# Experts fed in two batches, the first running through the last image's seam

## The reference, cut to what matters

```
x = x + conv(_ln_c(x))          # gate of three attentions: compressed, selected (top 16 blocks), windows 7x7
t = tokens(x)
t = t + ffn(_ln_t(t))
ffn(x):                         # N = 4096 tokens, D = 128, E = 8 experts, H = 512, TOP_K = 2
  logits = xt @ Wr + br
  top_p, top_idx = top_k(softmax(logits), 2);  weights = top_p / sum(top_p)
  xn = layernorm(xt)
  xe = xn * ln_g[e] + ln_b[e]
  h  = gelu(xe @ W1[e] + b1[e]);  y = h @ W2[e] + b2[e]
  out = sum over the two chosen experts of weight * y
```

## Time and profile before

| | us |
|---|---|
| median of three runs | 842.24 (840.95 to 847.28) |
| profiled execution, its own time | 840.26 |
| its span in the trace | 838.5 |
| PE busy | 666.8 (80%) |
| DVE busy | 514.0 (61%) |
| ACT busy | 418.8 (50%) |
| POOL busy | 239.5 (29%) |
| stretch of the expert tiles | 659 to 810 |
| PE busy in it | 146.72 of 151 |

### The profile page before, as it was taken

How to read it: one execution, slowest core, us unless ns; L and a number is a source line. 1 busy time by engine, 2 the same in 40 slices (tenths; PEclk the granted TensorE clock), 3 DMA queues, 4 the chain that set the end, 5 groups by cost and what they waited for, 6 DMA issues and landing times.

```text
span 838.5 us, 17744 instructions
## 1 busy us (share of the span) xinstructions
PE 666.8 (80%) x5228; PEld 500.0 (60%) x5229; DVE 514.0 (61%) x1719; ACT 418.8 (50%) x1238; POOL 239.5 (29%) x406
## 2 busy tenths in 40 slices
PE   2998899986889989688998966787631599999953
PEld 1684476654557556355755643553430599998952
DVE  4208378938857884875887568679763244444434
ACT  1327634663742554554356455326311388887842
POOL 3100043001013730201472010345015356565630
PEclk9999999997999999689999979957965799999985
DMA  9100000001000000000010170011022122222236
GB/s 315 58 1 26 1 6 1 2 1 51 2 1 5 27 27 6 21 0 2 5 33 20 34 195 0 4 37 42 2 76 64 48 64 63 69 63 63 63 128 219
DMA packets 34288, 38.63 MB, mean 46 GB/s; under 512 B 11668, under 2 KB 27044, under 8 KB 33956
## 3 DMA queue, kind: packets, MB, share of 16 engines
q1 hardware_dynamic: 28660, 26.77, 10.7%
q0 software_dynamic: 4416, 9.00, 3.0%
q10 hardware_dynamic: 1152, 2.10, 0.7%
HBM read 24.94 MB, written 13.98 MB: 46 GB/s over the span
## 4 chain that ended last, share of the span: by engine, by line
PE 52%; DVE 24%; issue 6%; ACT 6%; POOL 5%; DMA 4%; SPq 2%; DVEq 0%; POOLq 0%; ACTq 0%
PE ps L1919 7%; PE ps L1903 7%; PE ps L1483 6%; PE ps L1488 6%; PE ps L1537 5%; PE ps L1594 4%; DVE nmx L1060 4%; PE ps L1621 3%; DVE t_tok L1186 3%; DVE x_tok L1045 3%; PE ps L1552 3%; DVE r_P L1070 3%; PE ps L1524 2%; POOL xs_d L651 2%; DMA qTs<-z_d 2%
## 5 line engine op out<-in xcount | busy, mean ns | idle before, releaser
L783 ACT ACTIVATE r_P<-ps,nmx 128x225 f32<-128x225 f32 (+1 forms) x192 | 85.9, 467 | 58.2 <-DVE nmx L1060 58.2
L946 ACT ACTIVATE R<-ps,R 128x128 f32<-128x128 f32 x292 | 83.5, 368 | 44.9 <-PE ps L1903 44.9
L687 POOL DMA_INDIRECT z_d<-R x72 | 69.4, 964 | 67.1 <-DVE R L1445 49.8
L1483 PE MATMUL ps<-ident,r_P 128*128 128x128 f32 (+1 forms) x384 | 59.0, 291 | 32.7 <-ACT R L796 14.6
L574 POOL TENSOR_TENSOR rstd<-vpe,minus_half 128x8 f32<-128x8 f32 x8 | 13.3, 1658 | 236.7 <-DVE vpe L1006 236.7
L1483 PEld LDWEIGHTS ps<-ident,r_P 128*128 128x128 f32 (+1 forms) x384 | 47.0, 155 | 56.1 <-issue 29.1
L1919 PE MATMUL ps<-w_sb,R 128*128 x576 | 79.3, 280 | 0.0
L1060 DVE TENSOR_REDUCE nmx<-ps 128x4 f32<-128x900 f32 (+1 forms) x64 | 73.2, 1153 | 9.8 <-PE ps L1594 9.6
L1903 PE MATMUL ps<-R 128*128 128x128 f32 x584 | 78.9, 279 | 0.0
L1903 PEld LDWEIGHTS ps<-R 128*128 128x128 f32 x584 | 72.4, 195 | 0.0
L651 POOL DMA_INDIRECT xs_d<-pay,pos x64 | 63.0, 985 | 32.6 <-issue 18.9
(11 more groups left out here) (225 smaller groups left out, 1335.7 us busy)
## 6 DMA issues: line engine op xcount, KB each, us to landing
R<-xs_d SPq DMA_DIRECT2D x76, 65.0 KB, 1.8
x_sb<-x SPq DMA_DIRECT2D x4, 512.0 KB, 3.5
w_sb<-w1k SPq DMA_DIRECT2D x1, 2048.0 KB, 8.8
w_sb<-w1v SPq DMA_DIRECT2D x1, 2048.0 KB, 13.2
w_sb<-fw SPq DMA_DIRECT2D x1, 2048.0 KB, 9.9
w_sb<-fw SPq DMA_DIRECT2D x4, 512.0 KB, 10.5
out<-x_tok ACTq DMA_DIRECT2D x8, 256.0 KB, 2.3
t_d<-t_tok SPq DMA_DIRECT2D x3, 512.0 KB, 2.6
```

What stands on the lines that cost most here:

```text
L687: gp.indirect_dma_start(z_d, bass.IndirectOffsetOnAxis(wd[:, r, 1:2].bitcast(U32), 0), yrow[:, r, :], None).then_inc(y_out[r], 16)
L783: last = sc.activation(Pb[t % NRING][:, h, 0:m], bank(name)[:, (h % 2) * m:(h % 2) * m + m], ACT.Exp, bias=nmx[:, t % NRING, h:h + 1], acc ...
L946: last = sc.activation(hT[:, r % 2, c, :], hid(r)[:, C * c:C * c + C], ACT.Gelu, bias=wx[:, r, O_B1 + c:O_B1 + c + 1])
L1483: last = tr(bank(name)[0:m, k * j:k * j + k], src, ident[0:k, 0:k])
```

## The change

The two batches are images 0 and 1 (`BATCH[0]`) and images 2 and 3 (`BATCH[1]`). Each has its own region of `xs_d`, its own counts, table and padding, and 32 + 8 = 40 tiles; `NALL` = 80 tiles run in `NSTEP` = 83 steps. Step k turns tile k's rows, does the first layer of tile k−2 and the second layer of tile k−3. The loop is gone: every engine has the steps written out, and the fills of PSUM are in the plan. The table of batch 0 is made by DVE in the selected tiles of image 2. Steps 0 to 2 lie in the last three turns of image 3's selected tiles, step 3 behind its last output product, steps 4 to 7 between the projections, the rest of the seam and the router (PE: steps 13, 14, 18 and 22) between further steps. POOL scatters image 3's rows one per step in steps 19 to 34; tile 40 is the first of batch 1. Rows of images 0 to 2 are scattered two per selected tile of the next image. A row block's ring has 8 places, freed by the store of the tile 8 before, and POOL no longer copies the weight column: the store takes its indices from the row block. The results of images 0 and 1 are added and put out at steps 52 and 68, those of images 2 and 3 at the end. ACT still copies the weights, one tile ahead instead of two.

```diff
+SPLIT = 2
+BATCH = [list(range(SPLIT)), list(range(SPLIT, B))]
+CAP = [len(g) * N + 128 for g in BATCH]
+NTILE = [2 * len(g) * N // 128 + E for g in BATCH]
+NALL = sum(NTILE)
+Y_LAG, H_LAG = 3, 2
+W_AHEAD = 1
+XRING, WRING = 8, 4
+NSTEP = NALL + Y_LAG
+STEP_SEL, STEP_OS, STEP_TT, STEP_RT, STEP_RK, STEP_TAB = 0, 3, 13, 14, 18, 22
+def out_step(b):
+    return NTILE[0] + 12 + b * ((NTILE[1] - 8) // SPLIT)
...
 SyncE:
+            def tail_pads(q):
+                sp.wait_ge(tail_ready, q + 1)
+                for e in range(E):
+                    row = sp.value_load(tail_i[0:1, q, e:e + 1], min_val=0, max_val=sum(REGION) - 128)
+                    p0 = ((E + NPAD) * q + e) * 128
+                    sp.dma_start(xs_d[bass.ds(row, 128), :], pad_d[p0:p0 + 128, :]).then_inc(pad_in, 16)
+                sp.wait_ge(pad_in, 16 * (2 + E * (q + 1)))
+                sp.wait_ge(scattered, 16 * 2 * NT * (BATCH[q][-1] + 1))
+                sp.wait_ge(*copied(f"tb{q}"))
+            def load_rows(n):
+                k = n % XRING
+                if n >= XRING:
+                    sp.wait_ge(*row_stored(n - XRING))
+                row = sp.value_load(tab_i[0:1, 1, n:n + 1], min_val=0, max_val=sum(REGION) - 128)
                 sp.dma_start(xrow[:, k, :], xs_d[bass.ds(row, 128), :]).then_inc(xrow_in[k], 16)
...
+            tail_pads(0)
+            for n in range(NALL):
+                if n == NTILE[0]:
+                    tail_pads(1)
+                load_rows(n)
...
 GpSimd:
+            def scatter_rows(b):
+                for i in range(NT):
+                    pool.wait_ge(prob_ready, (b + 1) * 2 * NT + NT + i + 1)
+                    for j in (2 * i, 2 * i + 1):
+                        scatter_row(b, j // NT, j % NT)
+            def expert_step(k):
+                n = k - Y_LAG
+                if not 0 <= n < NALL:
+                    return
+                pool.wait_ge(y_ready, n + 1)
+                pool.nop(nofuse=True)
+                gp.indirect_dma_start(z_d, bass.IndirectOffsetOnAxis(xrow[:, n % XRING, C + 1:C + 2].bitcast(U32), 0),
+                                      yrow[:, n % XRING, :], None).then_inc(y_out[n % XRING], 16)
...
+            for k in range(STEP_OS + 7):
+                expert_step(k)
+            second_inverse_root(2 * B - 1, B - 1)
+            for k in range(STEP_OS + 7, STEP_RK + 1):
+                expert_step(k)
+            for k in range(STEP_RK + 1, NSTEP):
+                i = k - STEP_RK - 1
+                if i < 2 * NT:
+                    scatter_row(B - 1, i // NT, i % NT)
+                expert_step(k)
...
 ScalarE:
+            def expert_step(k):
+                if k + W_AHEAD < NALL:
+                    expert_weights(k + W_AHEAD)
+                n = k - H_LAG
...
+                act.wait_ge(*filled(f"fh{k}"))
...
+            def last_seam_and_experts(b):
+                for k in range(STEP_OS, NSTEP):
+                    if k == STEP_TT:
+                        for i in range(2):
+                            router_input(b, i)
+                        second_pay(b)
+                    if k == STEP_RT + 1:
+                        second_weight(b)
+                    expert_step(k)
+                    for i in BATCH[0]:
+                        if k == out_step(i):
+                            result(i)
...
 VectorE:
+            def expert_step(k):
+                name, n = f"fx{k}", k - Y_LAG
+                dve.wait_ge(*filled(name))
+                if 0 <= n < NALL:
...
+                    last = ve.tensor_tensor(yb[:, n % 2, :], bank(name)[:, 0:C], b2_all[:, bass.ds(e * C, C)], ALU.add)
+                if k < NALL:
+                    dve.wait_ge(wx_ready, k + 1)
...
+                    last = ve.tensor_scalar(xe[:, k % 2, :], bank(name)[:, C:2 * C], wx[:, k % WRING, O_G:O_G + 1],
+                                            wx[:, k % WRING, O_LB:O_LB + 1], ALU.mult, ALU.add)
+                last.then_inc(read_sem(name), 1)
+                if 0 <= n < NALL:
+                    if n >= XRING:
+                        dve.wait_ge(*row_stored(n - XRING))
+                    dve.wait_ge(*copied(name))
+                    ve.tensor_scalar(yrow[:, n % XRING, :], yb[:, n % 2, :], xrow[:, n % XRING, C:C + 1], None, ALU.mult)\
+                      .then_inc(y_ready, 1)
...
+            def last_seam_and_experts(b):
+                branch_output(b, "s", 1, osT)
+                expert_step(STEP_OS)
+                for q in range(4):
+                    combine(b, q)
+                    expert_step(STEP_OS + 1 + q)
+                k = STEP_OS + 5
...
+                row_sums(t_tok)
+                expert_step(k)
+                row_variances(EPS_T)
+                expert_step(k + 1)
+                expert_step(k + 2)
...
+                normalised(2 * b + 1, t_tok, xt_tok, xt_ready)
+                expert_step(k + 3)
+                payload(b)
...
 TensorE:
+            def expert_step(k):
+                n = k - H_LAG
+                if 0 <= n < NALL:
...
+                    pe.wait_ge(*copied(f"fx{n}"))
+                    claim(f"fh{k}")
+                    for c in range(HC):
+                        last = mm(bank(f"fh{k}")[:, C * c:C * c + C], wx[:, n % WRING, C * c:C * c + C], xe[:, n % 2, :],
+                                  start=True, stop=True)
+                    last.then_inc(full_sem(f"fh{k}"), 1)
+                n = k - Y_LAG
+                name = f"fx{k}"
...
+                if k < NALL:
+                    pe.wait_ge(*row_loaded(k))
+                    last = tr(bank(name)[:, C:2 * C], xrow[:, k % XRING, 0:C], ident[:, :])
+                if 0 <= n < NALL:
+                    pe.wait_ge(*copied(f"fh{n + H_LAG}"))
+                    for c in range(HC):
+                        last = mm(bank(name)[:, 0:C], hT[:, n % 2, c, :],
...
+                last.then_inc(full_sem(name), 1)
+            def result(b):
+                for j in range(2):
+                    pe.wait_ge(sum_ready, 2 * b + j + 1)
...
```

More of the change, by code:

```diff
@@ L109, in turned @@
             put(4 + k, f"T{s}{t}{'ab'[k]}@{b}")
+    late = around((6, 0, 1, 2, 3, 7, 4, 5))
     every = around(range(8))
@@ L1362, in seam @@
                 branch_output(b, "s", 1, osT)
-                combine(b)
+                for q in range(4):
+                    combine(b, q)
                 for t in range(4, NT):
@@ new lines, in result, with last_seam_and_experts @@
+            def result(b):
+                for j in range(2):
+                    pe.wait_ge(sum_ready, 2 * b + j + 1)
+                    transposes(f"out{j}@{b}", [zz[b % 2][0][:, 128 * (4 * j + q):128 * (4 * j + q) + 128] for q in range(4)], 128, 128)
+            def last_seam_and_experts(b):
+                branch_output(b, "s", 1, (128, 128))
+                expert_step(STEP_OS)
+                outputs_by_channels(b)
+                for q in range(4):
+                    for t in (2 * q, 2 * q + 1):
+                        branches_by_tokens(b, t)
+                    expert_step(STEP_OS + 1 + q)
+                for k in range(STEP_OS + 5, NSTEP):
+                    if k == STEP_TT:
+                        router_input(b)
+                    if k == STEP_RT:
+                        router_logits(b)
+                    if k == STEP_RK:
+                        ranks(b)
+                    if k == STEP_TAB:
+                        table_rows(1)
+                    expert_step(k)
+                    for i in BATCH[0]:
+                        if k == out_step(i):
+                            result(i)
+                for i in BATCH[1]:
+                    result(i)
@@ L1882, in _ @@
                 selected_tiles(b)
-                seam(b)
+                if b + 1 < B:
+                    seam(b)
+            last_seam_and_experts(B - 1)
             assert claimed == fills
-            for k in range(8):
-                pe.wait_ge(bank_read[k], fills[k] + 1)
-            mm(ps[:, 512 * 6:512 * 6 + E], ones[:, :], cum[:, NT, :], start=True, stop=True).then_inc(cnt_full, 1)
-            pe.wait_ge(tab_ready, 1)
-            for k in range(2):
-                last = mm(ps[0:1, 512 * 7 + 128 * k:512 * 7 + 128 * k + NTAB], tab[:, k:k + 1], ident[0:NTAB, 0:NTAB],
-                          start=True, stop=True)
@@ L1894, in _ @@
-            last.then_inc(tab_full, 1)
-            def turn_rows(r, loaded):
-                pe.wait_ge(xrow_in[r], loaded)
-                tr(turned(r), xrow[:, r, 0:C], ident[:, :]).then_inc(tr_full, 1)
-            def first_layer(r, n):
-                pe.wait_ge(xe_ready, n)
-                for c in range(HC):
-                    last = mm(hid(r)[:, C * c:C * c + C], wx[:, r, C * c:C * c + C], xe[:, r % 2, :], start=True, stop=True)
-                last.then_inc(h_full, 1)
-            turn_rows(0, 16)
@@ L2013 @@
     out = nc.dram_tensor("out", (B, C, N), F32, kind="ExternalOutput").ap()
```

(2 more changed lines are left out.)

586 lines of the change are left out of this document (302 added, 284 removed).

## The result

The changed kernel takes 847.28 us (median of 20 runs, 842.13 to 853.15), the kernel before 841.52 beside it (20 runs, 839.99 to 852.2): a ratio of 1.0056, 95% interval 1.0031 to 1.0081. Forecast were 829 and a range up to 846. The hole behind the last image is gone, as forecast, and nothing is won: the changed kernel is 0.56% slower, and the interval leaves out 1. Medians are over all runs; ratios leave out runs over 1.5% above the fastest of the same kernel. The profiled execution took 850.64 us, 3.4 above its median; its span is 848.8.

The account below looks back on a forecast made before the run. TensorE was taken to bound the expert tiles, with an unbound hole ahead. 608.9 + 163.9 + 4.5 + 7.4 + 14 + 7 = 805.7, + 19.6 = 825.3 against 838.5; as median 829 us, range 806 to 846.

Parts of the forecast that it names:

- VectorE's table of batch 1: Counts and table of batch 1, tiles 18 to 25: no VectorE term; only batch 0's table was priced, +4.2 us.
- Ahead of the tiles: Before the seam: batch 0's table +4.2 us, steps 0 to 2 about 1.5; last output product starts near 607.0, not 601.31.
- The pace: Steady tiles: 1.90 us each on PE without the loop, 80 tiles taking 152 us, less 1.2 done in steps 0 to 2.
- the pace stays at 2.06: Rival: slow tiles come from transfers, not the loop; 64 tiles take 0.16 us more each, +10, giving 839; chance 0.14.
- Seam work between tiles: Last seam and router placed between tiles: PE work 10 us, plus 4.5 of waits, bounds of the waits 0 to 9.
- Scatters in steps 19 to 34: Batch 1's scatters, one per step: GpSimd falls 10.6 us behind; less its idle and ring slack, PE loses 7.4, bounds 0 to 11.
- The border: Between batches at tile 40: eight tail pads on SyncE's queue stall PE 12 us, plus 2 for clock, bounds 8 to 16.
- Results between tiles: Results of images 0 and 1: PE waits for VectorE's sums, 3.5 us each, 7 in all, bounds 2 to 10; turns 2.1.
- Result loads: Loads of images 0 and 1's results among the tiles' row loads: priced at 0 outside the ring rival.
- The rival of the ring: Rival: slow store and load landings pace every step through the eight-place ring; 851 us at 3.5 beyond measured; chance 0.10.
- The end: After the last tile: only images 2 and 3 remain, the second result round goes, 30.9 us falling to 19.6.
- handovers hidden: Rival: neither scatters nor pads reach PE, so the 7.4 and 14 us terms fall away, giving 808; chance 0.14.

Follow-up runs that it names:

- ring of 12: Changed kernel with 12 row-block places instead of 8, stores' buffers left at 8: 830.28 us, ratio 0.9841 to the kernel before.
- pads early: Changed kernel with batch 1's tail pads issued behind row loads 28 to 35: 835.53 us, ratio 0.9874 to the kernel before.
- results at the end: Changed kernel with sums and outputs of images 0 and 1 moved behind step 82: 838.65 us, ratio 0.994 to the kernel before.
- the burst: Changed kernel with images 0 to 2 scattering 16 rows at once, as in the kernel before: 845.27 us, ratio 1.0043 to the kernel before.
- best version: Changed kernel with 12 row-block places, early tail pads and late results of images 0 and 1: 813.59 us, ratio 0.9659 to the kernel before, third set.
- first and third set: First four and last three follow-up experiments, each set beside its own runs of the kernel before; changed kernel's ratio 1.0056 and 1.0041.
- results two steps later: Changed kernel with 12 row-block places and early pads, TensorE and ScalarE handling results two steps after VectorE: 844.22 us, ratio 0.9658 to the kernel before.
- three edits: Changed kernel with 12 row-block places, early tail pads and results of images 0 and 1 behind step 82: 813.59 us in the third set.
- second set: Middle four follow-up experiments, all with two or three edits to the changed kernel, beside a kernel before that took 866.86 us.

## Why the prediction was wrong, step by step

The forecast was a gain of 13.2 us. The part that it counted as won came, but three terms of what is paid failed, all of them work or waits that now stand between tiles. The results of images 0 and 1, forecast at 9.1 (7 of waits, 2.1 of turns), took 15.1. The loads of these results on SyncE's queue, put at nothing for the ring of row blocks, stand in a stretch that took 7.3. VectorE's table of batch 1, put at nothing, is in a stretch that took 6.0.

The forecast put PE's last product at 805.7 on the profiled execution's clock; it ended at 828.8, 23.1 later. The steps give 4.9 + 6.6 − 0.6 − 1.5 + 7.3 + 6.0 = 22.7 of it.

*Ahead of the tiles, 4.9 late.* The last output product started at 611.9 and not at 607.0. Image 3's first compressed scores start 3.1 later than before, at 469.5 (4.2 forecast, for the table of batch 0), and steps 0 to 2 cost 1.2 (1.5). The other 6.3 lie between image 3's third compressed tile and its first selected scores: 77.6 us (from 492.4) and not 71.3 (from 489.3). In between PE, VectorE, ScalarE and GpSimd run as many instructions as before (536, 181, 108 and 22). The stretches 485 to 525 of before, of after and of the ring of 12 (columns as in the earlier trace rows):

```profile
485.00:525.00 40.00, 28.11 (x150) 16.74 (x151) 28.96 (x114) 22.88 (x85) 0.40 (x1) 0.83 0.30 77
```

```profile
485.00:525.00 40.00, 27.26 (x122) 17.90 (x123) 28.09 (x112) 21.64 (x78) 3.17 (x5) 0.72 0.00 1
```

```profile
485.00:525.00 40.00, 25.77 (x136) 15.83 (x140) 28.98 (x117) 23.94 (x87) 3.92 (x5) 0.85 0.00 1
```

The granted clock there is 0.83, 0.72 and 0.85. From the third compressed tile on it took 77.6 in the profiled execution with the pads early, 75.6 in the other one of the changed kernel and with the results at the end, 71.3 and 71.8 with the ring of 12 and with the burst. The best version was profiled twice, with 75.5 and with 71.3: one kernel has both. So these 6.3 are not a fixed cost of the edit, and they help the profiled execution to lie 3.4 above its median; without them it would have taken 844.3. Whether the change makes the long ones more frequent stays open. Of eleven profiled executions with the change six have 75.5 or more, of the two without it none, and while the medians of changed and before are 5.8 apart, their fastest runs are 2.1 apart (842.13 and 839.99).

*The pace: right.* 1.89 to 1.90 in every stretch without waits, so the rival "the pace stays at 2.06" fell. The rule of the Trainium skill on taken branches (Runtime: NRT & Kernel Launch, "Instruction fetch mechanics") was on the right side. But no run puts the loop back alone, so that the branch made the slow tiles is not shown.

*Seam work between tiles: right, but one piece was left out.* 15.1 against 14.5 for the seam and the router, as a sum; its pieces (10 of PE's work, 4.5 of waits) were not measured one by one. Batch 1's table was counted only with PE's own work. VectorE's part of it, priced at 4.2 for batch 0 and forgotten for batch 1, has no cover either (PE's timeline of the changed kernel):

```profile
664.39 1.16 PE L2032 MATMUL ps<-hk,wx 128*128 128x128 f32 x8 [0.71 <-DVE hk L1520]
...
668.87 0.30 PE L2019 MATMUL ps<-ident,tab 40*1 40x40 f32 x4 [2.31 <-DVE tab L1496]
669.10 1.48 PE L2032 MATMUL ps<-hk,wx 128*128 128x128 f32 x8
...
670.59 1.91 PE L2050 MATMUL ps<-w_sb,r_vc 128*128 x8
```

PE waits 2.31 for the table's columns, and the layers behind it take 1.48 and 1.91 instead of 1.06, at a granted clock of 0.50 from 670 to 672. The same place in the other profiled execution of the changed kernel:

```profile
666.22 0.30 PE L2019 MATMUL ps<-ident,tab 40*1 40x40 f32 x4 [2.31 <-DVE tab L1496]
...
667.56 1.06 PE L2050 MATMUL ps<-w_sb,r_vc 128*128 x8
```

The wait is the same and the granted clock stays at 1.00. Tiles 18 to 25 cost 6.0 in the first and 3.8 in the second (3.7 to 6.0 over all executions of the first and third set), so about 2.2 of the 6.0 come from the clock of that execution and not from the table's work.

*Scatters in steps 19 to 34: right, size and mechanism.* 6.8 against 7.4. The rule used was GpSimd's lag less the ring's slack; the stores' pitch of 2.53 was forecast at 2.56, and the ring of 12 takes the term to 0.1.

*The border: right.* 12.5 against 14, the wait 10.38 against 12. The pads alone, issued early, remove it.

*Results between tiles: the step that was mis-sized.* "3.5 each, 7 in all", plus 2.1 of turns; measured 15.1. Each wait was about as long as forecast (3.98 against 3.5; the forecast's own pieces, 1.1 and three times 0.65, make 3.05 and not its 3.2). What was left out is what follows it: the clock falls to its lower level, so the turns take 1.97, the next products 1.92 and 1.91 and the ones behind 1.20 instead of 1.06. The forecast added such a term at the border and not here. The results two steps later show it: without the wait 7.8 us less go there.

*Result loads: the step that was missing.* The forecast had the end's loads hidden and the rest of the ring slack at 1.8 to 2.3 us per place. The chain of waits of the changed kernel shows a row load of tile 49, behind the result loads of image 0:

```profile
739.71 0.51 SPq L591
...
741.20 4.15 DMA xrow<-xs_d
```

The load lands 4.15 us after its issue, where the earlier trace rows have 1.8, and the ring has no slack for that. Behind the result loads of image 1 (issued at 779.62) it is a store that lands late: issued at 780.43, it takes 4.95 us where the earlier trace rows have 2.23. The tiles directly behind the two pairs of loads (49 and 50, 65 to 67) lose 5.2 of the 7.3. The other 2.1 are mostly at tiles 61 and 77, where a store and a row load took 3.50 to land with no result load beside them; why is open. The ring of 12 takes the 7.3 to 1.2. The rival of the ring had this cause (result loads among the row loads) but priced it as a slower cadence over all steps, 22 us or nothing; it comes as a few stalls behind the loads. The three terms are 19.9 of the 23.1 (7.3, 6.0 above the forecast, 6.6 with the seam's 0.6).

*The end: right.* 19.6 forecast, 20.0 measured (828.8 to 848.8). With it the profiled execution is 23.5 above the 827.1 forecast for it.

The rival "handovers hidden" (808) was far off for this kernel; the three edits come within 6 us of it (813.6), but by moving the results too, which the rival left where they were.

What stays open: the unexplained waits in the second set; the varying stage of image 3; how much of the 3.8 to 6.0 us at tiles 18 to 25 is left if the table's columns are made a step earlier; and whether the ring would be needed if the result loads went out in smaller pieces. The last two were not tried.

## What to carry to other kernels

A gap that many small pieces of work used as cover is not won whole. List every piece that it hid (results, tables, pads, loads), and what each of them holds up once the gap is filled. Where one queue with a fixed order feeds a bound engine, anything of 10 us on that queue belongs tens of us ahead of its use, and the ring in front of the engine should be sized by the longest landing that occurs (4.15 and 4.95 here), not by the median one. Price a wait of a few us on TensorE in dense work with the slower products behind it, or hand over later, so that it does not wait.

## What the runs showed of the hardware

- Behind a wait of 3.98 us between dense products the granted clock was 0.50: the two sets of products behind it took 1.9 us instead of 1.06, and from 762 on the clock was 1.00 again. Behind a wait of 2.31 us it was 0.50 in one execution of the kernel and 1.00 in the other.
- The same stage took 71.3 and 75.5 us in two executions of one kernel, and 71.1 to 77.8 us over all thirteen. In 485 to 525 the granted clock was 0.83 to 0.87 in the executions with up to 73.7 us and 0.70 to 0.74 in those with 75.5 and more.
- A 65 KB load behind two 512 KB loads on the same queue took 4.15 us to land (median 1.8), and a store issued by GpSimd 0.8 us behind two others 4.95 (2.23). Single landings of 3.50 also occur without them.
- The indirect stores and scatters keep a pitch of 1.26 us on GpSimd in the scatter steps, and it is the same whether PE waits or not (stores 2.53 apart with 8 and with 12 places).
